# Maxima products of an attention kernel issued as pairs over half the rows, at fewer places, and a row sent without one of its waits

## The reference, cut to what matters

```python
q = x @ Wq.T + bq                       # x: layer-normalised, 32 x 56 x 128
k = context @ Wk.T + bk                 # context: 32 x 1500 x 128
v = context @ Wv.T + bv
scores = einsum('bhtd,bhcd->bhtc', q, k) / sqrt(8)
attn = softmax(scores, axis=-1)         # over the 1500 context rows
out = einsum('bhtc,bhcd->bhtd', attn, v) @ Wo.T + bo
x = x + tanh(g_xattn) * out
# then: sigmoid router, top 8 of 160, silu(x @ w_gate) weighted @ w_down, plus a shared expert
```

## Time and profile before

| | |
|---|---|
| median of 3 runs | 1141.21 us (1140.9 to 1142.85) |
| the profiled execution, its own time | 1140.58 us |
| its span in the trace | 1139.1 us |
| busy in the span: PE, DVE, ACT, POOL | 1069.6, 969.8, 845.1, 610.7 us |
| reductions of maxima (line 897) | 672, 420.9 us busy |
| maxima products (line 1203) | 672, 256.3 us busy |
| mean granted PE clock | 0.982 of full speed |

### The profile page before, as it was taken

How to read it: one execution, slowest core, us unless ns; L and a number is a source line. 1 busy time by engine, 2 the same in 40 slices (tenths; PEclk the granted TensorE clock), 3 DMA queues, 4 the chain that set the end, 5 groups by cost and what they waited for, 6 DMA issues and landing times.

```text
span 1139.1 us, 37969 instructions
## 1 busy us (share of the span) xinstructions
PE 1069.6 (94%) x12090; PEld 708.6 (62%) x12090; DVE 969.8 (85%) x1706; ACT 845.1 (74%) x1812; POOL 610.7 (54%) x1042
## 2 busy tenths in 40 slices
PE   2798899999999999999999999879999999999998
PEld 1366677777777777777777777644555555555554
DVE  3677788888888888888888888669999999999998
ACT  2566577777777777767777776658888888888886
POOL 4887888888888888888888988000000000000000
PEclk9799999999999999999999999889999999999999
DMA  6786866757667767568577552146777767776673
GB/s 129 162 179 150 187 155 171 170 137 182 154 143 184 156 161 176 135 159 180 139 182 164 132 144 61 25 138 209 231 226 232 239 227 226 234 236 226 225 240 115
DMA packets 201816, 197.06 MB, mean 173 GB/s; under 512 B 161999, under 2 KB 168207, under 8 KB 201782
## 3 DMA queue, kind: packets, MB, share of 16 engines
q1 hardware_dynamic: 188292, 174.14, 58.2%
q0 software_dynamic: 11520, 20.99, 6.5%
q10 hardware_dynamic: 1970, 1.49, 0.7%
HBM read 109.96 MB, written 12.55 MB: 108 GB/s over the span
## 4 chain that ended last, share of the span: by engine, by line
PE 45%; POOL 21%; issue 16%; DVE 9%; SPq 3%; DMA 2%; POOLq 2%; ACT 1%; DVEq 0%; ACTq 0%
PE bank L1368 15%; PE bank L1340 15%; PE bank L1170 4%; PE bank L1184 4%; DVE part_max L897 3%; POOL ctx_parts L495 3%; PE bank L1203 3%; POOL q_st L603 3%; POOL q_blk L585 3%; POOL w_in L468 3%; POOL w_in L470 2%; POOL w_out L516 2%; POOL w_out L515 2%; DVE rec L1024 2%; PE bank L1239 2%
## 5 line engine op out<-in xcount | busy, mean ns | idle before, releaser
L701 ACT ACTIVATE p_exp<-bank 125x448 f32<-125x448 f32 x768 | 400.2, 544 | 193.4 <-PE bank L1184 192.4
L897 DVE TENSOR_REDUCE part_max<-bank 128x1 f32<-128x500 f32 x672 | 420.9, 672 | 71.6 <-PE bank L1203 71.2
L1184 PE MATMUL bank<-q_st,k_stk 97*125 97x224 f16 x1536 | 275.6, 264 | 15.5 <-DMA q_st<-neg_row 8.9
L1203 PE MATMUL bank<-kparts,q_blk 128*128 128x500 f16 x672 | 256.3, 385 | 13.4 <-DVE part_max L897 11.2
L1184 PEld LDWEIGHTS bank<-q_st,k_stk 97*125 97x125 f16 x1536 | 197.2, 139 | 80.3 <-ACT p_exp L701 16.4
L1368 PE MATMUL bank<-ctT,w_ring 128*128 128x448 f16 x960 | 234.0, 353 | 3.0 <-DVE ctT L1072 3.0
L778 ACT ACTIVATE ctT<-bank 128x448 f32<-128x448 f32 x320 | 173.6, 543 | 40.6 <-PE bank L1340 16.1
L1072 DVE TENSOR_TENSOR ctT<-k_stk,ctT 128x448 f16<-128x448 f32 x320 | 198.2, 619 | 0.5 <-ACT ctT L784 0.4
L1170 PE MATMUL bank<-p_exp,v_sb 125*25 125x168 f32 (+1 forms) x6144 | 187.9, 263 | 0.4 <-ACT p_exp L701 0.4
L784 ACT ACTIVATE ctT<-k_stk 128x448 f16<-128x448 f32 x320 | 181.7, 568 | 5.5 <-DVE k_stk L1066 3.2
L1340 PE MATMUL bank<-q_hi,w_ring 128*128 128x448 f16 x640 | 174.0, 354 | 2.4 <-ACT k_stk L767 2.4
(11 more groups left out here) (157 smaller groups left out, 1241.1 us busy)
## 6 DMA issues: line engine op xcount, KB each, us to landing
v_sb<-c_scratch SPq DMA_DIRECT2D x114, 448.0 KB, 4.0
k_stk<-kparts SPq DMA_DIRECT2D x384, 93.8 KB, 3.5
ctx_in<-in_ctx_dram SPq DMA_DIRECT2D x30, 672.0 KB
k_stk<-c_scratch SPq DMA_DIRECT2D x38, 448.0 KB, 3.9
w_scratch<-w_out POOLq DMA_DIRECT2D x80, 128.0 KB, 3.2
w_in<-in_L_ffn_w_gate_dram POOLq DMA_DIRECT2D x160, 32.0 KB, 3.3
w_in<-in_L_ffn_w_down_dram POOLq DMA_DIRECT2D x80, 64.0 KB, 3.4
ctx_in<-in_ctx_dram SPq DMA_DIRECT2D x30, 78.0 KB
```

Source lines behind the costliest of these rows:

```text
L701: act.activation(p_exp[0:KP, j % PR, f * 448:(f + 1) * 448], ST[f][0:KP, 0:448], ACT.Exp).then_inc(exp_done, 1)
L897: v.reduce_max(part_max[:, i // NCH, i % NCH:i % NCH + 1], SM[i % NSM][:, 0:CK], axis=AX.X).then_inc(sm_maxed, 1)
L1184: last = pe.matmul(ST[f][0:KP, (g % 2) * GC:(g % 2 + 1) * GC], k_stk[0:97, u, g, j * KP:(j + 1) * KP], q_st[0:97, u, g, :, :].rearrange("p ...
L1203: pe.matmul(SM[i % NSM][:, 0:CK], rows, kparts[:, u, 0, c * CK:(c + 1) * CK], start=True, stop=True).then_inc(sm_done, 1)
```

## The change

A pair list replaces the counting rule. `ITEMS` says which (m, c) product i is, `PLACES` in which slot and place of the slot it stands. Nine pairs join a product of m = 0, 1, 2 with one of m = 4, 5, 6 on the same keys. The columns of m below 3 are those of heads 0 to 6, whose rows lie in 0 to 63; those of m above 3 belong to heads 9 to 15, whose rows lie in 64 to 127. Each of these eighteen products is now taken over its own 64 rows (`half_of`). The three products of m = 3 keep 128 rows. A third place exists now: 0 after the first two score products of a slot, 1 after the second two, 2 after the value products. Pairs stand at places 1 and 2 of slots 1, 3, 5, 7 and at place 1 of slot 9; the three whole products at place 0 of slots 2, 4 and 6. On DVE the reductions of places 0 and 1 come before the other work of the slot, those of place 2 after the copy of the value products. Independently, SP's sending of the row no longer waits for `qst_made`; PE's first score products of a sequence do.

```diff
+    LOWER, UPPER = slice(0, 64), slice(64, 128)
+    PAIRS = [((m, c), (m + MT // 2 + 1, c)) for c in range(NCH) for m in range(MT // 2)]
+    PAIRS_AT = [(1, 1), (1, 2), (3, 1), (3, 2), (5, 1), (5, 2), (7, 1), (7, 2), (9, 1)]
+    SINGLES_AT = [(2, 0), (4, 0), (6, 0)]
+    PLACED = sorted([(at, item) for at, pair in zip(PAIRS_AT, PAIRS) for item in pair] +
+                    [(at, (MT // 2, c)) for c, at in enumerate(SINGLES_AT)], key=lambda p: p[0])
+    PLACES, ITEMS = [at for at, _ in PLACED], [item for _, item in PLACED]
...
-        def chunks_at(k, place):
-            i = 2 * k + place
-            return [i] if i < MT * NCH else []
+        def items_at(k, place):
+            return [i for i, at in enumerate(PLACES) if at == (k, place)]
+        def half_of(m):
+            return LOWER if m < MT // 2 else UPPER if m > MT // 2 else slice(0, 128)
...
@@ SP
-                    sp.wait_ge(qst_made, b + 1)
                     sp.wait_ge(neg_copied, b + 1)
                     sp.dma_start(q_st[96:97, u, :, :, :]...
...
@@ DVE
-                    for i in chunks_at(k, 0) if on(step, 1) else []:
-                        maxima(step, i)
-                    for i in chunks_at(k, 1) if on(step, 1) else []:
-                        maxima(step, i)
+                    for place in (0, 1):
+                        for i in items_at(k, place) if on(step, 1) else []:
+                            maxima(step, i)
                     evacuate(step, k - 1)
                     if on(step, 3) and k == LAG:
...
                         v.tensor_copy(o_raw[:, :], OB[:, 0:OC]).then_inc(o_copied, 1)
+                    for i in items_at(k, 2) if on(step, 1) else []:
+                        maxima(step, i)
...
@@ PE, scores
                     pe.wait_ge(kst_here[u], h * (16 * 3 * HG) + 16 * 3 * HG)
+                    pe.wait_ge(qst_made, b + 1)
                     pe.wait_ge(row_here[u], h * 16 + 16)
...
@@ PE, maxima
-                rows = q_blk[:, u, :, :].rearrange("p a t -> p (a t)")[:, 128 * m:128 * m + 128]
-                pe.matmul(SM[i % NSM][:, 0:CK], rows, kparts[:, u, 0, c * CK:(c + 1) * CK],
+                rows = half_of(m)
+                heads = q_blk[rows, u, :, :].rearrange("p a t -> p (a t)")[:, 128 * m:128 * m + 128]
+                pe.matmul(SM[i % NSM][:, 0:CK], heads, kparts[rows, u, 0, c * CK:(c + 1) * CK],
                           start=True, stop=True).then_inc(sm_done, 1)
...
@@ PE, body
                         if scores_there:
                             scores(bs, js, f)
-                        for i in chunks_at(k, 0) if f == 0 and on(step, 1) else []:
+                        for i in items_at(k, f) if on(step, 1) else []:
                             maxima(step, i)
...
-                    for i in chunks_at(k, 1) if on(step, 1) else []:
+                    for i in items_at(k, 2) if on(step, 1) else []:
                         maxima(step, i)
```

More of the change, by code:

```diff
@@ L896, in maxima @@
                 dve.wait_ge(sm_done, b * (MT * NCH) + (i + 1))
-                v.reduce_max(part_max[:, i // NCH, i % NCH:i % NCH + 1], SM[i % NSM][:, 0:CK],
+                m, c = ITEMS[i]
+                v.reduce_max(part_max[:, m, c:c + 1], SM[i % NSM][:, 0:CK],
                              axis=AX.X).then_inc(sm_maxed, 1)
@@ L1192, in maxima @@
                 b = num(back(step, 1))
-                m, c = i // NCH, i % NCH
+                m, c = ITEMS[i]
                 if i == 0:
```

## The result

| | before | changed |
|---|---|---|
| median of the runs | 1141.62 us | 1184.56 us (1181.45 to 1186.96) |
| ratio | | 1.0376 [1.036, 1.0393] |
| profiled execution / its span | 1140.6 / 1139.1 us | 1181.45 / 1179.9 us |
| two steps in the middle of the attention, transpose to transpose | 41.34 us | 44.60 us |
| transpose of the fifth step / of the last | 148.08 / 711.72 | 146.21 / 749.77 |

A forecast was written before the change was run, and what follows sets the result against it. A loop of waits between PE and DVE bounds the step: 20.9 + 0.7 + 0.2 = 21.8 us. Over 27 steps with router work +29.0, row -2.4: +26.6 on 1140.6 is 1167.2, median 1168; range 1148 to 1190.

The forecast's parts named there:

- the ring through DVE: Attention step: product i waits for maximum i-3; this loop of PE and DVE becomes the bound, 20.9 us; chance 0.65.
- rival 1: Maxima pairs on PE: the two products run one after the other, about 22.5 us a step, 1187 us; chance 0.18.
- from the first product of a step to the last: Path taken for the DVE loop: product 0 to product 20 through maximum 17, then PE's way back; 20.9 us.
- its 5.9: PE's stretch after the change from the last pair, slot 9, to the next step's first, slot 1: 5.9 us.
- 0.7 in all: Slots 10, 11 and 0, bare of maxima products: PE's score waits for ACT, 0.2 to 0.3 us each, 0.7 together.
- the 0.2 for DVE: Third bank running dry twice a step, in slots 5 and 7: costs DVE 0.2 us.
- the 4 us for the router's work: Router's copies on DVE, in slots that are full after the change, count whole: 4 us over the 27 steps.
- DVE has 2.4 us to spare: Kernel before: the loop through DVE takes 18.3 us, under PE's 20.67 a step, leaving DVE 2.4 us.
- PE's own 19.4: PE's work per step after the change, with pairs side by side: 20.4 - 1.9 + 0.4 + 0.5 = 19.4 us.
- half the price of the changes: Added changes of form between scores and pairs on PE, 9 x 0.09 = 0.8 us a step, counted at half.
- The row: Row sent without `qst_made`: at 131.28 saves 2.0 us of transfer and 1.6 of clock; with slower step, -2.4 us.
- Rival 2: DVE keeps pace, POOL's 41.28 us for two steps is the bound: faster, 1134 us; chance 0.11.

The follow-up runs named there:

- before_bank: The kernel before with POOL's stores issued later and the reciprocal left in its bank for the multiplication to read: 1132.76 us, ratio 0.9946.
- row_alone: The kernel before with only the row edit (SP sends the row without waiting for `qst_made`, PE's scores wait instead): 1145.32 us, ratio 1.0038.
- pair_moved: The changed kernel with slot 7's second pair, the one behind the reciprocal, moved to slot 9: 1147.07 us, ratio 1.0055.
- the copy: The changed kernel with a copy in place of DVE's reciprocal, which is left out of the computation: 1145.54 us, ratio 1.0051.
- pairs_spread: The changed kernel with its nine pairs and three whole products spread evenly over slots 0 to 10: 1148.99 us, ratio 1.0069.
- before_stores_later: The kernel before with POOL's store and the load behind it issued after the next split: 1139.43 us, ratio 0.9988.

## Why the forecast came out as it did

- **The side and the mechanism** held: the ring through DVE took over, POOL waits for PE, PE waits for maxima in slots 5 and 7.
- **The size did not, and the range was partly luck.** 1184.56 lies outside the 1157 to 1179 that the forecast gave its own case. It lies in the stated range only because that was widened to take in rival 1, whose mechanism did not happen.
- **The step that went wrong: "from the first product of a step to the last".** The forecast took the ring from product 0 to product 20 by way of maximum 17, and counted the wait of product 18 behind the reciprocal, "1.1 us inside the ring", as part of it. The ring that sets the step closes at product 18 by way of maximum 15: maximum 17 is taken by 430.96, and product 20, in the pair at 431.46, does not wait for it. At the forecast's own prices the two rings are equally long: 0.38 + 16 x 0.61 + 0.94 + 1.90 + 0.12 = 13.1 up to product 18, from there 0.31 + 0.39 + 0.70 + 0.39 + 0.09 = 1.9 to slot 9's pair, and its 5.9, which make 20.9. So the wrong product alone did not move the sum; it hid which waits count.
- **Two terms were too small.** PE's way from product 18 to the next first pair is 8.74 in the mean (9.21 and 8.27) and not 7.8: "0.7 in all" for ACT's waits measured 0.9, and 0.28 of it is in the stretch that this ring has more than the other (430.70 to 431.46, 0.76 for four scores whose own time is 0.48). From the first pair to product 18 it is 13.56 in the mean (13.44 and 13.68) and not 13.1: the 0.2 for DVE measured 0.5. In it are the waits for slot 3's pair (0.45 and 0.23) and, in most second steps, 0.36 from the collision with POOL, which the forecast put at nothing. 20.9 + 0.9 + 0.5 is 22.3.
- **What the 16.6 us are made of.** Between the transposes, 27 steps at 0.5 more are 13.5; of the 4 us for the router's work only 1.5 showed (603.56 against 27 x 22.30 = 602.1), 2.5 less. Up to the fifth transpose 0.5 more came than forecast, behind the last 2.8, and the median lies 3.1 and not 0.6 above the profiled execution. The stretch behind the last transpose is 425.9 to 430.1 us in these kernels with the same experts, so nothing is to be read into the 2.8.
- **"DVE has 2.4 us to spare"** was wrong of the kernel before, and one of its own rows shows it: the product at 433.31 waits 0.25 us for the maximum behind the multiplication, and it does so in every step of before_bank too, where POOL waits for TensorE. The ring by way of the reciprocal was closed before the change, with no time to spare.
- **PE's own 19.4** was too good: right that pairs run side by side (0.31), wrong in "half the price of the changes". A change costs 0.09 to 0.12, whole. In the even places a pair saves 0.04 us, 0.4 us a step, not 1.0; without any wait a step of pairs is 19.98.
- **The row**: -2.4 by the fifth transpose was forecast, -1.9 came, with the clock at 1.00. That the gain stays until the end was only assumed; alone it did not. POOL's `q_st` is done at 129.35 and the first scores start at 129.54, 0.2 and not 0.1 behind it.
- **Rival 2**, faster, came true only after three more changes: even places, POOL's stores later, the reciprocal in its bank. It set the condition as 1.2 us less in the ring. pair_moved and the copy took that off, but off 22.3 and not off 21.8, and came to 21.0, not to 20.64; in pairs_spread the ring was out of the way and POOL, lengthened by its collisions, stood at 41.64 and not at 41.28. Rival 1 is refuted by the 0.31.

What stays open: why the median of row_alone is 4 us over its profiled execution, whether the early row costs at the start of the changed kernel, what the pauses of POOL are, and why some steps of the changed kernel have the collision and others not.

## What to carry to other kernels

With a ring of n buffers, every product closes a ring of its own: sum the loop for each of them, above all for the one whose buffer comes free behind the longest foreign instruction, and take the longest, with the waits of both engines for a third one in it. If one product waits in every step before the change, that ring has no time to spare, whatever the sum says. Halving the rows of a product pays only if the halves run in pairs and if few changes of form are paid for it: count 0.1 us for each change before counting the 0.1 to 0.2 us that a pair saves, and put the pairs where a form changes anyway. When two engines hold one pace, taking work off one only shows the next; and an edit can cost time simply by moving an instruction onto one of another engine.

## What the runs showed of the hardware

- Two products over different 64 rows, into different banks, 500 columns each: 0.31 us together, as for one 64-row product alone before another form; 0.21 for one over 128 rows. A change between 64-row, 97-row and 128-row forms adds 0.09 to 0.12 us, where scores of 97 rows and products of 128 rows follow each other at no extra cost.
- A DVE multiplication of two SBUF operands (128x224, 0.39 us) beside an instruction of POOL that reads SBUF takes up to 1.31 us, and POOL's small conversions take 0.45 instead of 0.29. With one operand in a bank it took 0.39 all 32 times.
- The start differs too: in before_bank the wait for the row, 3.03 us in the earlier trace rows, is the 0.29 in this row of PE's timeline,

```profile
...
126.85 0.40 PE L1193 MATMUL bank<-q_st,k_stk 97*125 97x224 f16 x2 [0.29 <-DMA q_st<-neg_row]
...
```

and the fifth transpose comes at 142.06; in before_stores_later, with the same POOL program, the wait was 3.19. These two traces do not tell why they differ.
